# GpSimd's block sums of the next x wait for both normalised tiles of h

## The reference, cut to what matters

```python
# x: (64, 256, 512) float32, adj: (256, 256) of 0 and 1
mi, mj = x @ Wi.T, x @ Wj.T                        # W = [Wi | Wj], 512 x 1024
g = deg * (mi + b) + adj @ mj                      # deg: row sums of adj
h = layernorm(x + g)
q, k, v = h @ Wq.T + bq, h @ Wk.T + bk, h @ Wv.T + bv   # 8 heads of 64
p = softmax(where(adj == 0, -inf, q @ k.T / 8))
out = layernorm(h + (p @ v) @ Wo.T + bo)
```

## Time and profile before

| what | value |
|---|---|
| median of 3 runs | 3001.79 us (3000.93 to 3002.13) |
| profiled execution | 3026.84 us, its span 3024.9 us |
| PE busy in the span | 2903.7 us (96%) |
| DVE busy | 2377.9 us (79%) |
| POOL busy | 1877.5 us (62%) |
| ACT busy | 1862.6 us (62%) |
| granted TensorE clock, mean | 0.995 |
| matmul of 128x512 / of 128x256, typical | 0.40 us / 0.28 us |

### The profile page before, as it was taken

How to read it: one execution, slowest core, us unless ns; L and a number is a source line. 1 busy time by engine, 2 the same in 40 slices (tenths; PEclk the granted TensorE clock), 3 DMA queues, 4 the chain that set the end, 5 groups by cost and what they waited for, 6 DMA issues and landing times.

```text
span 3024.9 us, 59823 instructions
## 1 busy us (share of the span) xinstructions
PE 2903.7 (96%) x18584; PEld 2456.9 (81%) x18584; DVE 2377.9 (79%) x6029; ACT 1862.6 (62%) x4874; POOL 1877.5 (62%) x1793
## 2 busy tenths in 40 slices
PE   7999999999999999999999999999999999999997
PEld 5888888888788888888887888888888878878886
DVE  7787787877877878878778778787787787787876
ACT  4666656656666566666666665665666666656664
POOL 4666666666566666666665665666666666656563
PEclk9999999999999999999999999999999999999998
DMA  4333333333323333323333233332332332332321
GB/s 137 101 105 98 111 97 104 104 97 104 100 95 111 97 104 110 98 97 108 100 104 99 95 111 97 100 108 97 104 104 95 106 104 97 111 97 97 105 92 55
DMA packets 282404, 306.71 MB, mean 101 GB/s; under 512 B 18816, under 2 KB 214912, under 8 KB 282368
## 3 DMA queue, kind: packets, MB, share of 16 engines
q1 hardware_dynamic: 282368, 306.26, 31.2%
HBM read 173.55 MB, written 132.64 MB: 101 GB/s over the span
## 4 chain that ended last, share of the span: by engine, by line
PE 46%; DVE 24%; issue 16%; POOL 8%; ACT 5%; DVEq 1%; POOLq 0%; DMA 0%; SPq 0%; ACTq 0%
PE proj L493 25%; PE av L493 7%; PE proj L611 6%; DVE probs L1036 5%; PE attn L655 4%; ACT probs L820 4%; PE proj L530 3%; DVE oT L1087 3%; DVE exp_bias L1043 3%; DVE xb L1113 2%; POOL pT_lo L397 2%; DVE xb L1119 2%; PE attn L670 1%; DVE v_both L990 1%; POOL probs L388 1%
## 5 line engine op out<-in xcount | busy, mean ns | idle before, releaser
L820 ACT ACTIVATE probs<-probs,exp_bias 128x256 f32<-128x256 f32 x1024 | 508.6, 498 | 342.2 <-DVE exp_bias L1043 342.1
L388 POOL TENSOR_TENSOR probs<-probs,row_inv 128x512 f32<-128x512 f32 x256 | 266.5, 1041 | 476.6 <-DVE row_inv L1053 476.6
L1036 DVE CUSTOM_DVE_ANT_0 probs<-attn,mask_add 128x256 f32<-128x256 f32 x1024 | 381.1, 419 | 148.0 <-PE attn L655 147.7
L397 POOL TENSOR_TENSOR pT_lo<-pT_raw,pT_hi 128x512 fp32r<-128x512 f32 x315 | 402.9, 1296 | 149.2 <-ACT pT_hi L851 148.9
L530 PE MATMUL proj<-wji_hi,xs_hi 128*128 128x512 f32 x896 | 382.3, 427 | 24.7 <-DVE xb L1113 11.8
L530 PE MATMUL proj<-wji_hi,xs_lo 128*128 128x512 f32 x896 | 355.4, 397 | 0.0
L530 PE MATMUL proj<-wji_lo,xs_hi 128*128 128x512 f32 x896 | 355.3, 397 | 0.0
L611 PE MATMUL proj<-mj_hi,wq_hi 128*128 128x256 f32 x1024 | 293.5, 287 | 26.3 <-DVE mj_lo L990 26.3
L493 PE MATMUL av<-pT_hi,v_both 128*128 128x256 f32 x1016 | 266.1, 294 | 47.3 <-DVE oT L1087 29.1
L1144 DVE TENSOR_SCALAR hb<-hb,mean_var_out,rstd_out 128x512 f32<-128x512 f32 x128 | 122.3, 996 | 226.9 <-POOL rstd_out L415 226.9
L420 POOL TENSOR_TENSOR oT_lo<-oT,oT_hi 128x256 fp32r<-128x256 f32 x256 | 194.4, 759 | 151.7 <-ACT oT_hi L864 151.6
(11 more groups left out here) (125 smaller groups left out, 8824.5 us busy)
## 6 DMA issues: line engine op xcount, KB each, us to landing
bounce<-probs SPq DMA_DIRECT2D x189, 512.0 KB, 2.6
pT_raw<-bounce SPq DMA_DIRECT2D x756, 128.0 KB, 3.1
xs_raw<-in_xT SPq DMA_DIRECT2D x64, 512.0 KB, 4.1
xb<-in_x SPq DMA_DIRECT2D x64, 512.0 KB, 3.4
out<-hb SPq DMA_DIRECT2D x64, 512.0 KB, 2.8
w_raw<-in_w0T SPq DMA_DIRECT2D x8, 256.0 KB, 6.0
stage<-in_wqT SPq DMA_DIRECT2D x1, 1024.0 KB, 9.8
stage<-in_wkT SPq DMA_DIRECT2D x1, 1024.0 KB, 11.6
```

The lines of the kernel that those rows point to most:

```text
L388: pool.tensor_tensor(e, e, inv, ALU.mult).then_inc(norm_odd_done, 1)
L397: pool.tensor_tensor(pT_lo[:, g % 2, :, :, i, :, :], pT_raw[:, g % 2, :, :, i, :, :], pT_hi[:, :, :, i, :, :].bitcast(F32), ALU.subtract). ...
L820: last = nc.scalar.activation(e, e, ACT.Exp, bias=exp_bias[:, g % 2, s:s + 1], scale=SCALE, accum_out=row_sum[:, g % 2, s:s + 1])
L1036: last = V.tensor_tensor_reduce(out=out_, in0=in_, in1=mask_, scale=1.0, scalar=MASKED, op0=ALU.add, op1=ALU.max, accum_out=row_max[:, g % ...
```

## The change

The sums of batch n wait until `normed["h"]` has reached R * n. In `step(b)` the call is `sum_x(b + 2)`, so the wait is for R(b + 2): both tiles of h of batch n = b + 1, which is the `norm_apply` of the same step. In the prologue `sum_x(1)` stands right behind a wait for the same value.

```diff
@@ block.gpsimd
             def sum_x(n):
+
+                pool.wait_ge(normed["h"], R * n)
                 pool.wait_ge(xT_loaded, 16 * (n + 1))
                 x_ = lambda i: xs_raw[:, i, :, :]
                 pool.tensor_tensor(x_(4), x_(0), x_(3), ALU.add).then_inc(xs_summed, 1)
```

## The result

| | before | changed |
|---|---|---|
| median of 12 runs | 3001.18 us (2999.34 to 3002.73) | 2992.25 us (2989.53 to 2996.40) |
| ratio to before | | 0.9971, 95% interval 0.9962 to 0.9980 |
| profiled execution, its span | 3026.84, 3024.9 us | 2993.06, 2991.2 us |

The change makes the kernel 8.9 us or 0.3% faster. The forecast was 2991 us. Where the kernel before loses the race of `exp_bias(b, 3)` often, the gain is larger: in a later set of runs the same two kernels took 3033.03 and 2992.51 us.

A forecast was written before the change was run, and what follows sets the result against it. TensorE bounds it, busy 45.11 of 45.89 us a step. Profiled 3026.84 - 26.8 (lost races) - 9.3 (chain) = 2990.7; plain 3001.79 - 9.3 = 2992.5 without races; forecast 2991 us, own range 2987 to 2995, overall 2982 to 3003.

The forecast's parts named there:

- the race of `exp_bias(b, 3)`: VectorE's exp_bias(b, 3) against GpSimd's second p_low(b, 1): 1.07 us per lost step, 25 of 62 lost in the profile.
- The port term: Normalisation of h, line 1144: with the sums held, both tiles take 1.64 us, not 2.06, ending 0.42 earlier.
- the step without sums: The step starting at 2952.42 in the profile before, without GpSimd's sums; its 1.64 us normalisation served as model.
- What arrives: TensorE's attend(b, 1) starts at 7.68 in place of 7.83: 0.15 us a step, 9.3 us in all.
- The 1.7 lost races: exp_bias(b, 3) races assumed lost in plain runs before, none after; moved the forecast from 2992.5 to 2990.7 us.
- The cost of the held back sums: GpSimd's sums start at 1.73, end at 4.6, before p_low(b, 1) at 5.09: no cost.
- The cover: GpSimd's idle time ahead of p_low(b, 1): 1.06 us before, expected near 0.5 after.
- The margin of the race: exp_bias(b, 3) leads the second p_low(b, 1) by 80 ns, where it was within 10; won in all steps.
- The reading of 3026.84 against 3001.79: Profiled against plain time: recording causes 25 lost races, 26.8 us; plain runs lose one or two of 62.
- Hidden anyway: Chain behind TensorE's transposes set by something else: gain at most 4.3 us or nothing, 2997 to 3002; chance 0.18.
- Slower: exp_bias(b, 3) loses in each step, 3057 us (3024 if half), or sums outlast 5.09, 3005; chance 0.13.
- More than forecast: Plain runs lose 6 to 12 races before, none later: another 5 to 11 us, 2980 to 2986; chance 0.10.

The follow-up runs named there:

- the first set: One of three sets of runs, on one chip: the unchanged kernel before took 3033.03 us (17 runs), the changed kernel 2992.51 us.
- the two kernels without a race: The kernel before and the changed kernel, each with exp_bias of head pair 3 made by ScalarE: 2999.34 and 2989.17 us.
- the second set: Another of the three sets of runs, on one chip: the unchanged kernel before took 3000.43 us (21 runs).
- third: The last of the three sets of runs, on one chip: the unchanged kernel before took 3000.06 us (21 runs).

## Why the prediction was right, and where not

**The port term was right.** Line 1144 went to 1.64 us as the step without sums had shown, and the run that waits for the first tile only shows the mechanism: whoever of the two engines comes first makes the other wait.

**What arrives was right within 0.03 us a step.** 0.15 us were forecast; the pairs of traces give 45.87 - 45.75 = 0.12 for the first, 0.14 for the first set, and 0.14 between the two kernels without a race. With 62 steps these are 7 to 9 us, and the medians differ by 8.9. The 1.7 lost races that brought the forecast from 2992.5 to 2991 are not shown: in the second set the kernel before became 1.1 us faster without the race, one race's worth and within the noise. Holding `normalise_odd` too showed that TensorE's own start, not the normalisation, is the limit beyond that.

**The cost of the held back sums was right, a bit too small.** I had the first sum at 1.73 and the last end at 4.6, and they were at 1.81 and 4.75. The 0.08 belong to the one register instruction that the wait brings in the loop; in the step at 2873.19, which is written out, the first sum starts at 1.72. The cover was 0.32 us and not 0.5, and the run that waited for `y_sum` shows what lies behind it.

**The margin of the race was wrong.** I read 80 ns from the step without sums. That step is written out, and the loop's steps have register instructions on VectorE ahead of the maxima: in them `exp_bias(b, 3)` starts at 6.32, not at 6.26, only 4 to 14 ns ahead of the second `p_low`. The written out steps of the changed kernel do have 80 ns, but those of the kernel before have 55 to 66 already, so most of the 80 was never the change's. No race was lost in either trace of the changed kernel, but with such leads that was not by margin: this part of the forecast came true, but by luck as far as the runs tell. Nor do the starts tell who wins at this distance. In the rows of the prediction `exp_bias` led by 3 ns in the short step and by 6 in the long one, so "decided by some 10 ns" names a near tie and no more. I compared two steps that differ in more than the sums, and put all of the difference down to them. The same mistake did no harm at `attend(b, 1)`, where GpSimd and not VectorE decides.

**The reading of 3026.84 against 3001.79 was half right.** That lost races make the difference is borne out by the step counts in both traces: 24 x 1.08 = 25.9 us, and 3026.84 is 25.7 above the 12 runs' median. (The prediction counted 25 by the waits, one of which is no lost race.) That the recording causes them is not: in the first set every run of the kernel before was long, in the second and third none was. The profiled execution of 3026.84 us isn't among those 12 runs, while that of every other kernel here is among its own. Whether the chip or something else of a set decides it was not separated; each of the three sets had one chip. Why leads of 5 to 10 ns were lost in more than half of the steps in the first set, while the changed kernel lost none with leads of 3 to 20 ns on the same chip, stays open too. The Trainium skill (Runtime: NRT & Kernel Launch, The ~15µs preamble/postamble breakdown) puts some 6.2 us between a profile's time and a plain one. No run here can test that, since the profiled execution of the changed kernel, 2993.06 us, is itself one of the 12 behind the median of 2992.25. The lower forecast that the prediction worked out by it, near 2985, didn't come true.

**The rivals.** "Hidden anyway" named the right limit at the transposes, TensorE's 0.07, but the chain behind them carried more, 0.14. "Slower" had the right mechanism for the sums: they outlast their cover if held 0.6 us longer. "More than forecast" came true in a way that I hadn't meant, in a set of runs in which the kernel before loses about 30 races and the change gains 40 us.

## What to carry to other kernels

Where VectorE and GpSimd work beside each other, look for short VectorE instructions with long records: a `tensor_scalar` of four columns that takes 0.9 us where 0.17 is its free time is waiting for GpSimd's instruction to end. Hold back the GpSimd work that nobody needs yet, or move such small instructions to ScalarE, and price it by the steps in the trace where the neighbour is missing, comparing loop steps with loop steps. When you bound what TensorE can win, add up the waits of its weight loads too, not its matmuls' alone.

## What the runs showed of the hardware

The exclusion goes by whole instructions and both ways: `exp_bias` of 128x4 took 0.17 us free and 1.33 behind a `p_low` of 1.29, and a sum of 128x256 took 0.89 behind the second tile and 0.73 free. The Trainium skill (SBUF — State Buffer, Who interferes with whom) says so of VectorE in its two-port modes, which a `tensor_scalar` can enter: whoever issues first has the shared pair of ports for its whole instruction. The trace agrees in these durations; the mode itself no row shows. How a near tie ends is another matter: at leads of 5 to 10 ns the same instruction pair went both ways, in 35 of 62 steps against VectorE in one trace.

A further finding is the price of idle TensorE: with a wait of up to 1.8 us once a step the granted clock fell from 2.4 to 1.2 GHz in 26 of 62 steps, and the matmuls behind took 1.5 us more, nearly as much as the wait itself. The other 36 steps had the same wait and kept the clock; what tells them apart was not found. The waits of 1.2 us that the kernel before has in the same place when it loses a race never brought it down.
